# Attention with one exp per query block in place of two halves, and four buffers in place of two in the statistics pass

## The chip, the cores and the metric

The kernel runs as one program on all 8 cores of one Trainium2 chip. Each core computes 1024 tokens of the output; nothing is exchanged between cores. The metric is the device time of the slowest core in microseconds (us).

## What is computed

One transformer layer in which attention and a mixture of experts both read the same normalised input and are added to it. Cut to what matters:

```python
xn = layernorm(x)                                  # x: (4, 2048, 2048) f32
# attention, H = 16 heads of HD = 128, G = 4 key/value groups (head h uses group h % 4)
qkv = xn @ Wqkv + bqkv
scores = einsum('bqhd,bkhd->bhqk', q, k) / HD
prob = softmax(scores, axis=-1)                    # over 2048 keys
attn = einsum('bhqk,bkhd->bqhd', prob, v) @ Wout + bout
# 32 experts of width 768, top 8 of a softmax gate, with a threshold
for each expert e: acc += (silu(xn @ Wg[e].T) * (xn @ Wu[e].T)) @ Wd[e].T * combine[:, e]
out = x + attn + acc
```

## The kernel before

Each core owns 1024 tokens of one sequence (x_own) and also reads the other 1024 (x_nbr), for keys and values. Every engine has its own instruction list in program order; semaphores written out by hand order them (one counter each for TensorE, VectorE and ScalarE, `st`, `sv`, `ss`, and one per DMA buffer). On VectorE and ScalarE each instruction also waits for the one before it. The stages, in order:

1. **Statistics pass** (L286 to L300). For 16 tiles of 128 tokens: SP loads 128x2048 f32 (1 MB) into one of the two buffers `xtile`, VectorE sums it (L296), ScalarE squares it with a running sum into PSUM that nobody reads (L299). SP may refill a buffer when both engines are done with the tile two back. L302 to L318 then turn the 16 sums into mean and scale with small VectorE instructions and one square root.
2. **Normalising pass** (L422 to L531). The same 16 tiles are loaded again, normalised by ScalarE (L439, L443), transposed on TensorE (L457, L482) and copied out; the gate's logits (L498), then the QKV matmuls (L351).
3. **Attention** (L596 to L732), 128 blocks i = (head h, query block q of 128), eight blocks a head. `ps_a` is four banks of PSUM, 128x2048 f32, one block's scores against all 2048 keys. For block i the engines are given:
   - TensorE: scores of the keys 0 to 1023 (L616) once the first exp of block i-1 is done, scores of 1024 to 2047 (L627) once the second exp is done; in every eighth block the 32 P·V matmuls of the head before (L703); then 16 transposes of the normalised block i-2 into `ps_b` (L675).
   - VectorE: the copy of `ps_b` into `pnT` for block i-2 (L689), then, for block i, the add of the two halves' sums (L651), a running offset (L657), a reciprocal (L659), and the normalising multiply into `pn_sb` (L662).
   - ScalarE: where P·V was done, its two copies out (L712); the exp of the first half (L643) and of the second (L647), each with an accumulated row sum, which costs an accumulator read behind it; then Ln of the whole sum (L654), for which it waits on VectorE's add. Offset and `p_exp` are double buffered: the exp of block i waits for VectorE's L657 and L662 of block i-2.
4. **Output projection** (L753) and the **expert stage** (L858 to L931), the bulk of the time: gate and up matmuls (L895), down matmuls (L831) with weights streamed by GpSimd's queue.
5. The final transposes, the residual and the store.

`B.barrier()` stands between attention and its neighbours: all engines wait for TensorE, VectorE and ScalarE. GpSimd's queue issues nothing during attention; SP's issues nothing either.

Of the kernel before, what the change touches and what calls it, by code (L numbers as in the profile page):

```python
# [102 lines left out]
def build_program():  # L103
# [18 lines left out]
    def sb(name, shape, dtype, off):  # L122
        return nc.alloc_sbuf_tensor_at(name, shape, dtype, offset=MBASE + off).ap()
# [23 lines left out]
    sm = Small(8192, 16384)  # L147
# [12 lines left out]
    nmax128 = sm.get("nmax128", 1)  # L160
    ssum = sm.get("ssum", 1)
    ssum2 = [sm.get("ssum2a", 1), sm.get("ssum2b", 1)]
    ssb2 = [sm.get("ssb2a", 1), sm.get("ssb2b", 1)]
    lns2 = [sm.get("lns2a", 1), sm.get("lns2b", 1)]
    nmax2 = [sm.get("nmax2a", 1), sm.get("nmax2b", 1)]
    rssum = sm.get("rssum", 1)
# [22 lines left out]
    sumx_all = sm.get("sumx_all", 16)  # L189
    sumx2_all = sm.get("sumx2_all", 16)  # L190
# [19 lines left out]
    xtile = [sb(f"xtile{i}", [128, D], F32, DYN + i * 8192) for i in range(2)]  # L210
# [38 lines left out]
    ps_a = nc.alloc_psum_tensor("ps_a", [128, 2048], F32).ap()  # L249
# [4 lines left out]
    B = Builder(nc)  # L254
# [17 lines left out]
    ev_xdma = [None] * 16  # L272
    ev_red1 = [None] * 16
    ev_sq1 = [None] * 16
# [8 lines left out]
    ev_cT = [None] * 16  # L283
    ev_cTev = [None] * 16

    for t in range(16):  # L286
        own = t < 8
        buf = t % 2
        src_ = dx_own if own else dx_nbr
        row = (t % 8) * 128  # L290
        if t >= 2:
            B.wait("sync", "sv", ev_red1[t - 2])
            B.wait("sync", "ss", ev_sq1[t - 2])
        ev_xdma[t] = B.dma("sync", xtile[buf][:], src_[row:row + 128, :], f"sxt{buf}")
        B.wait("vector", f"sxt{buf}", ev_xdma[t])
        ev_red1[t] = B.op("vector", lambda e, b=buf, t=t: e.reduce_sum(  # L296
            sumx_all[:, t:t + 1], xtile[b][:], axis=AX.X), "sv")
        B.wait("scalar", f"sxt{buf}", ev_xdma[t])
        ev_sq1[t] = B.op("scalar", lambda e, b=buf, t=t: e.activation(  # L299
            ps_a[:, 0:2048], xtile[b][:], AF.Square, accum_out=sumx2_all[:, t:t + 1]), "ss")  # L300

    B.wait("vector", "ss", ev_sq1[15])  # L302
    B.op("vector", lambda e: e.tensor_scalar_mul(mean_all[:], sumx_all[:], 1.0 / D))
# [118 lines left out]
    for t in range(16):  # L422
        own = t < 8
        buf = t % 2
        src_ = dx_own if own else dx_nbr
        row = (t % 8) * 128
        if t >= 2:
            B.wait("sync", "ss", ev_xn_done[t - 2])
        else:
            B.wait("sync", "sv", ev_red1[14 + t])  # L430
            B.wait("sync", "ss", ev_sq1[14 + t])
        ev_xdma[t] = B.dma("sync", xtile[buf][:], src_[row:row + 128, :], f"sxt{buf}")

        B.wait("scalar", f"sxt{buf}", ev_xdma[t])
        if t >= 2:
            B.wait("scalar", "st", ev_tpb[t - 2][1])
            if t - 2 < 8:
                B.wait("scalar", "st", ev_tpf[t - 2][1])
        ev_xnbf[t] = B.op("scalar", lambda e, b=buf, t=t: e.activation(  # L439
            xnbf[b][:], xtile[b][:], AF.Identity,  # L440
            bias=negmr_all[:, t:t + 1], scale=rstd_all[:, t:t + 1]), "ss")
        if own:
            ev_xnf[t] = B.op("scalar", lambda e, b=buf, t=t: e.activation(  # L443
                xnf[b][:], xtile[b][:], AF.Identity,
                bias=negmr_all[:, t:t + 1], scale=rstd_all[:, t:t + 1]), "ss")
# [147 lines left out]

    B.barrier()

    ev_expAC = [None] * 128  # L596
    ev_expBC = [None] * 128
    ev_normC = [None] * 128
    ev_biasC = [None] * 128
    ev_tpC = {}  # L600
# [7 lines left out]
    def emit_scores(i):  # L608
        h, q = divmod(i, 8)
        g = h % G  # L610
        if i >= 1:
            B.wait("tensor", "ss", ev_expAC[i - 1])

        def sc_mm01(e, h=h, q=q, g=g):
            for kb in range(2):
                ins = e.matmul(ps_a[:, kb * 512:(kb + 1) * 512],  # L616
                               q_sb[:, h * TOWN + q * 128: h * TOWN + q * 128 + 128],
                               k_sb[:, g * S + kb * 512: g * S + kb * 512 + 512],
                               start=True, stop=True)
            return ins  # L620
        ev01 = B.op("tensor", sc_mm01, "st")
        if i >= 1:
            B.wait("tensor", "ss", ev_expBC[i - 1])

        def sc_mm23(e, h=h, q=q, g=g):
            for kb in (2, 3):
                ins = e.matmul(ps_a[:, kb * 512:(kb + 1) * 512],  # L627
                               q_sb[:, h * TOWN + q * 128: h * TOWN + q * 128 + 128],
                               k_sb[:, g * S + kb * 512: g * S + kb * 512 + 512],
                               start=True, stop=True)  # L630
            return ins
        ev23 = B.op("tensor", sc_mm23, "st")
        return (ev01, ev23)

    def emit_softmax(i, ev_sc):
        qb2 = i % 2
        B.wait("scalar", "st", ev_sc[0])
        if i >= 2:
            B.wait("scalar", ev_normC[i - 2][0], ev_normC[i - 2][1])
            B.wait("scalar", "sv", ev_biasC[i - 2])  # L640
        else:
            B.wait("scalar", "sv", ev_nz)
        ev_expAC[i] = B.op("scalar", lambda e, qb2=qb2: e.activation(  # L643
            p_exp[qb2][:, 0:1024], ps_a[:, 0:1024], AF.Exp, bias=nmax2[qb2][:],
            accum_out=ssum2[qb2][:]), "ss")
        B.wait("scalar", "st", ev_sc[1])
        ev_expBC[i] = B.op("scalar", lambda e, qb2=qb2: e.activation(  # L647
            p_exp[qb2][:, 1024:2048], ps_a[:, 1024:2048], AF.Exp, bias=nmax2[qb2][:],
            accum_out=ssb2[qb2][:]), "ss")
        B.wait("vector", "ss", ev_expBC[i])  # L650
        ev_stot = B.op("vector", lambda e, qb2=qb2: e.tensor_tensor(  # L651
            ssum2[qb2][:], ssum2[qb2][:], ssb2[qb2][:], ALU.add), "sv")
        B.wait("scalar", "sv", ev_stot)
        ev_ln = B.op("scalar", lambda e, qb2=qb2: e.activation(  # L654
            lns2[qb2][:], ssum2[qb2][:], AF.Ln), "ss")
        B.wait("vector", "ss", ev_ln)
        ev_biasC[i] = B.op("vector", lambda e, qb2=qb2: e.tensor_tensor(  # L657
            nmax2[qb2][:], nmax2[qb2][:], lns2[qb2][:], ALU.subtract), "sv")
        B.op("vector", lambda e, qb2=qb2: e.reciprocal(rssum[:], ssum2[qb2][:]))  # L659
        if (i - 2, 1) in ev_tpC:  # L660
            B.wait("vector", ev_tpC[(i - 2, 1)][0], ev_tpC[(i - 2, 1)][1])
        ev_normC[i] = ("sv", B.op("vector", lambda e, qb2=qb2: e.tensor_scalar_mul(  # L662
            pn_sb[qb2][:], p_exp[qb2][:], rssum[:]), "sv"))
# [194 lines left out]
    for e in range(NE):  # L858
        B.wait("tensor", f"ssel{e % 2}", ev_sel[e])
        for hfi in range(2):  # L860
            if ev_crep_psfree is not None:
# [4 lines left out]
                start=True, stop=True), "st")  # L866
# [167 lines left out]
```

How the kernel before makes its waits and increments, by code:

```python
    def op(self, eng, fn, inc=None, n=1):  # L43
        auto = self.SELF_SEM.get(eng)
        if auto is not None:
            assert inc in (None, auto), (eng, inc)
            self.wait(eng, auto, self.cnt[auto])
            inc = auto
            n = 1
        if inc is None:
            self.streams[eng].append(lambda e, fn=fn: fn(e))
            return None
        self.cnt[inc] += n
        sem = self.sems[inc]
        self.streams[eng].append(
            lambda e, fn=fn, sem=sem, n=n: fn(e).then_inc(sem, n))
        return self.cnt[inc]
# [4 lines left out]
    def wait(self, eng, semname, val):  # L62
        if val is None or val <= 0:
            return
        self.streams[eng].append(
            lambda e, s=self.sems[semname], v=val: e.wait_ge(s, v))
```

## Time and profile before

| | us |
|---|---|
| three runs, median | 5870.77 |
| lowest, highest | 5581.49, 6046.8 |
| the profiled execution | 5581.49 |
| its span, slowest core (core 4) | 5579.6 |
| spans of the eight cores | 5564.0 to 5579.6 |
| mean granted TensorE clock of the cores | 0.955 to 0.958 |

The profiled execution is the lowest of the three. All rows come from core 4 of it. A row of the timeline is start and duration in us, engine, line, operation, output<-inputs, and in brackets how long the engine sat idle before it and what ended that. PE is TensorE, PEld its weight loads, DVE VectorE, ACT ScalarE. The end of a matmul row is modelled. The granted clock is a share of full speed, and a few matmul records can be missing (a group of 32 may be listed as x31).

### The profile page before, as it was taken

What the parts mean: (1) busy time and instruction counts of PE and PEld (TensorE: products, weight loads), DVE (VectorE), ACT (ScalarE), POOL (GpSimd) and SP (SyncE); (2) the same over time, 40 slices, a digit from 0 to 9 for tenths busy, and PEclk for the clock granted to TensorE, in tenths of its full rate; (3) what the DMA queues carried; (4) which work ended last, traced back from release to release, by engine and by line L of the source; (5) the groups of instructions that cost most, each with busy time, mean ns of one, the idle gap of its engine ahead of it and who ended that gap; (6) DMA issues with size and microseconds to landing.
All of it is one profiled execution on the core that took longest, in us unless ns stands there. A gap on an engine that the chain in (4) does not pass through costs nothing.

```text
span 5579.6 us, 64195 instructions; the slowest of 8 cores (5564.0 to 5579.6 us)
## 1 busy us (share of the span) xinstructions
PE 5010.6 (90%) x23550; PEld 2328.6 (42%) x24008; DVE 1741.9 (31%) x2616; ACT 792.5 (14%) x1301; POOL 261.6 (5%) x497
## 2 busy tenths in 40 slices
PE   3875666678999999999999999999999999999995
PEld 2532333333444444444444444444444444444443
DVE  3002566630233322222222233332222222223333
ACT  4221555531000000000000000000000000000000
POOL 0000000000000000000000000000000000000000
PEclk9787999989999999999999999999999999999997
DMA  5231000016434444444444433434444444444333
GB/s 172 73 75 31 1 1 1 1 21 105 76 68 75 74 73 79 72 75 73 74 74 72 76 72 69 78 71 77 75 72 76 72 76 72 75 74 72 68 63 123
DMA packets 80462, 380.45 MB, mean 68 GB/s; under 512 B 9760, under 2 KB 10912, under 8 KB 65824
## 3 DMA queue, kind: packets, MB, share of 16 engines
q0 software_dynamic: 70992, 325.12, 33.0%
q1 hardware_dynamic: 9168, 51.21, 2.7%
q8 instruction: 201, 3.29, 0.2%
q14 instruction: 101, 0.83, 0.1%
HBM read 693.00 MB, written 8.39 MB: 126 GB/s over the span
## 4 chain that ended last, share of the span: by engine, by line
PE 83%; DVE 8%; issue 3%; DMA 3%; ACT 2%; DVEq 0%; ACTq 0%; SPq 0%; POOLq 0%
PE ps_a L895 48%; PE ps_d L831 23%; PE ps_a L351 4%; DVE pn_sb L662 2%; DVE pnT L689 2%; PE ps_d L703 2%; PE ps_a L753 2%; PE ps_b L863 1%; PE ps_b L498 1%; DMA x_re<-x_own 1%; DMA wgubuf<-gu 1%; PE ps_b L457 1%; PE ps_d L482 0%; ACT p_exp L647 0%; DMA xtile<-x_own 0%
## 5 line engine op out<-in xcount | busy, mean ns | idle before, releaser
L895 PE MATMUL ps_a<-xn_own,wgubuf 128*128 128x512 bf16 x12044 | 2692.8, 384 | 24.6 <-DMA wgubuf<-gu 10.8
L895 PEld LDWEIGHTS ps_a<-xn_own,wgubuf 128*128 128x128 bf16 x12288 | 1211.4, 99 | 1517.4 <-issue 103.7
L831 PE MATMUL ps_d<-hstash,wdbuf 128*128 128x512 bf16 x6016 | 1330.5, 379 | 11.1 <-DVE ffn_acc L841 0.9
L918 DVE TENSOR_TENSOR sg_sb<-ps_a,sg_sb 128x512 f32<-128x512 f32 x384 | 265.6, 692 | 2408.2 <-PE ps_a L895 2408.2
L831 PEld LDWEIGHTS ps_d<-hstash,wdbuf 128*128 128x128 bf16 x6144 | 596.0, 97 | 741.5 <-issue 181.8
L841 DVE TENSOR_TENSOR ffn_acc<-ffn_acc,ps_d 128x512 f32<-128x512 f32 x1024 | 703.8, 687 | 606.7 <-PE ps_d L831 603.0
L908 ACT ACTIVATE sg_sb<-ps_a 128x512 f32<-128x512 f32 x384 | 229.3, 597 | 2260.1 <-PE ps_a L895 2260.1
L60 POOL DMA_DIRECT2D wgubuf<-gu x384 | 203.5, 530 | 2602.6 <-PE ps_a L895 2546.8
L923 DVE TENSOR_TENSOR hstash<-sg_sb,c_rep 128x512 bf16<-128x512 f32 x384 | 266.0, 693 | 39.9
L873 ACT ACTIVATE c_rep<-ps_b 128x512 f32<-128x512 f32 x64 | 38.2, 597 | 1534.9 <-PE ps_b L863 1485.8
L689 DVE COPY pnT<-ps_b 128x2048 bf16<-128x2048 bf16 x128 | 156.7, 1224 | 115.2 <-PE ps_b L675 103.3
L351 PE MATMUL ps_a<-xn_own,wjbuf 128*128 128x512 bf16 x750 | 181.4, 404 | 2.4 <-issue 1.8
L616 PE MATMUL ps_a<-k_sb,q_sb 128*128 128x512 bf16 x214 | 75.0, 419 | 110.4 <-ACT p_exp L643 108.0
L662 DVE TENSOR_SCALAR pn_sb<-p_exp,rssum 128x2048 bf16<-128x2048 f32 x128 | 164.6, 1286 | 14.5 <-DVE rssum L659 1.2
L675 PE MATMUL ps_b<-ident_b,pn_sb 128*128 128x128 bf16 x2048 | 149.5, 231 | 17.2 <-DVE pnT L689 8.0
L675 PEld LDWEIGHTS ps_b<-ident_b,pn_sb 128*128 128x128 bf16 x2048 | 131.4, 104 | 71.1 <-issue 64.2
L627 PE MATMUL ps_a<-k_sb,q_sb 128*128 128x512 bf16 x256 | 81.6, 402 | 80.5 <-ACT p_exp L647 80.5
L457 PE MATMUL ps_b<-ident_b,xnbf 128*128 128x128 bf16 x256 | 30.2, 291 | 124.1 <-ACT xnbf L439 107.9
L703 PE MATMUL ps_d<-pnT,vt_sb 128*128 128x512 bf16 x501 | 125.9, 411 | 8.0 <-DVE ssum2b L651 4.8
L351 PEld LDWEIGHTS ps_a<-xn_own,wjbuf 128*128 128x128 bf16 x768 | 79.2, 104 | 101.8 <-issue 24.3
L753 PE MATMUL ps_a<-attn_o,woutbuf 128*128 128x512 bf16 x502 | 113.1, 386 | 7.3 <-DMA woutbuf<-wout 6.7
L351 PE MATMUL ps_a<-xn_nbr,wjbuf 128*128 128x512 bf16 x251 | 58.0, 389 | 55.4 <-DMA wjbuf<-wqkv 55.0
(106 smaller groups left out, 1302.4 us busy)
## 6 DMA issues: line engine op xcount, KB each, us to landing
wgubuf<-gu POOLq DMA_DIRECT2D x384, 512.0 KB, 5.0
wdbuf<-down POOLq DMA_DIRECT2D x64, 1536.0 KB, 10.8
xtile<-x_own SPq DMA_DIRECT2D x16, 1024.0 KB, 5.2
xtile<-x_nbr SPq DMA_DIRECT2D x16, 1024.0 KB, 5.7
wjbuf<-wqkv POOLq DMA_DIRECT2D x28, 512.0 KB, 6.1
woutbuf<-wout POOLq DMA_DIRECT2D x16, 512.0 KB, 5.3
x_re<-x_own SPq DMA_DIRECT2D x8, 1024.0 KB, 6.9
o<-out_sb SPq DMA_DIRECT2D x8, 1024.0 KB, 4.8
```

The source lines that it names most:

```text
L351: ins = e.matmul(ps_a[:, bank * 512:(bank + 1) * 512], wjbuf[use][:, dc * 128:(dc + 1) * 128], xn_mv(dc, tblk), start=(dc == 0), stop=(dc ...
L662: ev_normC[i] = ("sv", B.op("vector", lambda e, qb2=qb2: e.tensor_scalar_mul(pn_sb[qb2][:], p_exp[qb2][:], rssum[:]), "sv"))
L675: ins = e.matmul(ps_b[:, k * 1024 + j * 128: k * 1024 + (j + 1) * 128], pn_sb[qb2][:, kc * 128:(kc + 1) * 128], ident_b[:], is_transpose=True,
L689: e.tensor_copy(d, s), "sv")
L703: ins = e.matmul(pv_ps, vt_sb[:, (g * 16 + kc) * 128:(g * 16 + kc) * 128 + 128], pnT[:, kc * TOWN + qb * 512: kc * TOWN + qb * 512 + 512], ...
L753: ins = e.matmul(ps_a[:, bank * 512:(bank + 1) * 512], woutbuf[oc % 2][:, dic * 128:(dic + 1) * 128], attn_o[:, dic * TOWN + tblk * 512: d ...
L831: ins = e_.matmul(ps_d[:, slot * 512:(slot + 1) * 512], wdbuf[gh % 3][:, (dc % 8) * 768 + icc * 128: (dc % 8) * 768 + icc * 128 + 128], hs ...
L841: e_.tensor_tensor(ffn_acc[:, dc * TOWN + tb * 512: dc * TOWN + tb * 512 + 512], ffn_acc[:, dc * TOWN + tb * 512: dc * TOWN + tb * 512 + 512],
L895: ins = e_.matmul(ps_a[:, bank * 512:(bank + 1) * 512], wgubuf[bufi][:, dc * 128:(dc + 1) * 128], xn_own[:, dc * TOWN + tb * 512: dc * TOW ...
L908: ev_silu[(e, ip, tb)] = B.op("scalar", lambda e_, tb=tb: e_.activation(sg_sb[:, tb * 512:(tb + 1) * 512], ps_a[:, tb * 512:(tb + 1) * 512 ...
L918: ev_h1[(e, ip, tb)] = B.op("vector", lambda e_, tb=tb: e_.tensor_tensor(sg_sb[:, tb * 512:(tb + 1) * 512], ps_a[:, (2 + tb) * 512:(3 + tb ...
L923: e_.tensor_tensor(hstash[e2 % 2][:, ip * TOWN + tb * 512: ip * TOWN + tb * 512 + 512], sg_sb[:, tb * 512:(tb + 1) * 512], c_rep[e2 % 2][: ...
```

## The change

Three edits.

- **Statistics pass.** Two more 1 MB buffers, `xp1a` and `xp1b`, laid over memory that the normalising pass uses later (`xnf1` and `xnTf0`), join `xtile`; tile t goes to buffer t % 4, each with its own semaphore, and SP waits for the tile four back. The first two reloads of the normalising pass wait for tiles 12 and 13, and ScalarE's first normalise also waits for the last reduction.
- **Scores.** The two groups of two matmuls per block become one of four, which waits for the whole exp of the block before.
- **Softmax.** The two exps of 1024 columns become one of 2048 with one accumulated sum; the second sum, VectorE's add and ScalarE's wait for it are gone.

```diff
--- before.py
+++ after.py
@@ -160,7 +160,6 @@
     nmax128 = sm.get("nmax128", 1)
     ssum = sm.get("ssum", 1)
     ssum2 = [sm.get("ssum2a", 1), sm.get("ssum2b", 1)]
-    ssb2 = [sm.get("ssb2a", 1), sm.get("ssb2b", 1)]
     lns2 = [sm.get("lns2a", 1), sm.get("lns2b", 1)]
     nmax2 = [sm.get("nmax2a", 1), sm.get("nmax2b", 1)]
     rssum = sm.get("rssum", 1)
@@ -219,6 +218,9 @@
     act_all = sb("act_all", [128, 8 * NE], F32, 193536)
     scr_all = sb("scr_all", [128, 8 * NE], F32, 194560)
     fb_all = sb("fb_all", [128, 8 * NE], F32, 195584)
+    xp1 = [None, None,
+           sb("xp1a", [128, D], F32, 49152),
+           sb("xp1b", [128, D], F32, 57344)]
     xn_own = sb("xn_own", [128, DC * TOWN], BF16, 73728)
     xn_nbr = sb("xn_nbr", [128, DC * TOWN], BF16, 106496)
 
@@ -283,21 +285,23 @@
     ev_cT = [None] * 16
     ev_cTev = [None] * 16
 
+    xp1[0], xp1[1] = xtile[0], xtile[1]
+    p1sem = ["sxt0", "sxt1", "sxr0", "sxr1"]
     for t in range(16):
         own = t < 8
-        buf = t % 2
+        buf = t % 4
         src_ = dx_own if own else dx_nbr
         row = (t % 8) * 128
-        if t >= 2:
-            B.wait("sync", "sv", ev_red1[t - 2])
-            B.wait("sync", "ss", ev_sq1[t - 2])
-        ev_xdma[t] = B.dma("sync", xtile[buf][:], src_[row:row + 128, :], f"sxt{buf}")
-        B.wait("vector", f"sxt{buf}", ev_xdma[t])
+        if t >= 4:
+            B.wait("sync", "sv", ev_red1[t - 4])
+            B.wait("sync", "ss", ev_sq1[t - 4])
+        ev_xdma[t] = B.dma("sync", xp1[buf][:], src_[row:row + 128, :], p1sem[buf])
+        B.wait("vector", p1sem[buf], ev_xdma[t])
         ev_red1[t] = B.op("vector", lambda e, b=buf, t=t: e.reduce_sum(
-            sumx_all[:, t:t + 1], xtile[b][:], axis=AX.X), "sv")
-        B.wait("scalar", f"sxt{buf}", ev_xdma[t])
+            sumx_all[:, t:t + 1], xp1[b][:], axis=AX.X), "sv")
+        B.wait("scalar", p1sem[buf], ev_xdma[t])
         ev_sq1[t] = B.op("scalar", lambda e, b=buf, t=t: e.activation(
-            ps_a[:, 0:2048], xtile[b][:], AF.Square, accum_out=sumx2_all[:, t:t + 1]), "ss")
+            ps_a[:, 0:2048], xp1[b][:], AF.Square, accum_out=sumx2_all[:, t:t + 1]), "ss")
 
     B.wait("vector", "ss", ev_sq1[15])
     B.op("vector", lambda e: e.tensor_scalar_mul(mean_all[:], sumx_all[:], 1.0 / D))
@@ -427,11 +431,13 @@
         if t >= 2:
             B.wait("sync", "ss", ev_xn_done[t - 2])
         else:
-            B.wait("sync", "sv", ev_red1[14 + t])
-            B.wait("sync", "ss", ev_sq1[14 + t])
+            B.wait("sync", "sv", ev_red1[12 + t])
+            B.wait("sync", "ss", ev_sq1[12 + t])
         ev_xdma[t] = B.dma("sync", xtile[buf][:], src_[row:row + 128, :], f"sxt{buf}")
 
         B.wait("scalar", f"sxt{buf}", ev_xdma[t])
+        if t == 0:
+            B.wait("scalar", "sv", ev_red1[15])
         if t >= 2:
             B.wait("scalar", "st", ev_tpb[t - 2][1])
             if t - 2 < 8:
@@ -593,8 +599,7 @@
 
     B.barrier()
 
-    ev_expAC = [None] * 128
-    ev_expBC = [None] * 128
+    ev_expC = [None] * 128
     ev_normC = [None] * 128
     ev_biasC = [None] * 128
     ev_tpC = {}
@@ -609,48 +614,28 @@
         h, q = divmod(i, 8)
         g = h % G
         if i >= 1:
-            B.wait("tensor", "ss", ev_expAC[i - 1])
-
-        def sc_mm01(e, h=h, q=q, g=g):
-            for kb in range(2):
+            B.wait("tensor", "ss", ev_expC[i - 1])
+
+        def sc_mm(e, h=h, q=q, g=g):
+            for kb in range(4):
                 ins = e.matmul(ps_a[:, kb * 512:(kb + 1) * 512],
                                q_sb[:, h * TOWN + q * 128: h * TOWN + q * 128 + 128],
                                k_sb[:, g * S + kb * 512: g * S + kb * 512 + 512],
                                start=True, stop=True)
             return ins
-        ev01 = B.op("tensor", sc_mm01, "st")
-        if i >= 1:
-            B.wait("tensor", "ss", ev_expBC[i - 1])
-
-        def sc_mm23(e, h=h, q=q, g=g):
-            for kb in (2, 3):
-                ins = e.matmul(ps_a[:, kb * 512:(kb + 1) * 512],
-                               q_sb[:, h * TOWN + q * 128: h * TOWN + q * 128 + 128],
-                               k_sb[:, g * S + kb * 512: g * S + kb * 512 + 512],
-                               start=True, stop=True)
-            return ins
-        ev23 = B.op("tensor", sc_mm23, "st")
-        return (ev01, ev23)
+        return B.op("tensor", sc_mm, "st")
 
     def emit_softmax(i, ev_sc):
         qb2 = i % 2
-        B.wait("scalar", "st", ev_sc[0])
+        B.wait("scalar", "st", ev_sc)
         if i >= 2:
             B.wait("scalar", ev_normC[i - 2][0], ev_normC[i - 2][1])
             B.wait("scalar", "sv", ev_biasC[i - 2])
         else:
             B.wait("scalar", "sv", ev_nz)
-        ev_expAC[i] = B.op("scalar", lambda e, qb2=qb2: e.activation(
-            p_exp[qb2][:, 0:1024], ps_a[:, 0:1024], AF.Exp, bias=nmax2[qb2][:],
+        ev_expC[i] = B.op("scalar", lambda e, qb2=qb2: e.activation(
+            p_exp[qb2][:], ps_a[:], AF.Exp, bias=nmax2[qb2][:],
             accum_out=ssum2[qb2][:]), "ss")
-        B.wait("scalar", "st", ev_sc[1])
-        ev_expBC[i] = B.op("scalar", lambda e, qb2=qb2: e.activation(
-            p_exp[qb2][:, 1024:2048], ps_a[:, 1024:2048], AF.Exp, bias=nmax2[qb2][:],
-            accum_out=ssb2[qb2][:]), "ss")
-        B.wait("vector", "ss", ev_expBC[i])
-        ev_stot = B.op("vector", lambda e, qb2=qb2: e.tensor_tensor(
-            ssum2[qb2][:], ssum2[qb2][:], ssb2[qb2][:], ALU.add), "sv")
-        B.wait("scalar", "sv", ev_stot)
         ev_ln = B.op("scalar", lambda e, qb2=qb2: e.activation(
             lns2[qb2][:], ssum2[qb2][:], AF.Ln), "ss")
         B.wait("vector", "ss", ev_ln)
```

## Rows read from the trace of the kernel before

**Rows 1.** The page: the chain that ended last, share of the span by line.

```profile
PE ps_a L895 48%; PE ps_d L831 23%; PE ps_a L351 4%; DVE pn_sb L662 2%; DVE pnT L689 2%; PE ps_d L703 2%; PE ps_a L753 2%; PE ps_b L863 1%; PE ps_b L498 1%; DMA x_re<-x_own 1%; DMA wgubuf<-gu 1%; PE ps_b L457 1%; PE ps_d L482 0%; ACT p_exp L647 0%; DMA xtile<-x_own 0%
```

**Rows 2.** Statistics pass: groups by line, landing times, timeline, a window's busy times.

```profile
L296 DVE TENSOR_REDUCE sumx_all<-xtile 128x1 f32<-128x2048 f32 x16 | 36.6, 2286 | 31.5 <-DMA xtile<-x_own 17.2 <-DMA xtile<-x_nbr 14.3
L299 ACT ACTIVATE ps_a<-xtile 128x2048 f32<-128x2048 f32 x16 | 30.1, 1881 | 29.1 <-DMA xtile<-x_nbr 16.1 <-DMA xtile<-x_own 12.9
...
DMA to landing us min/median/max: 4.8/5.4/10.7
...
12.20 2.29 DVE L296 TENSOR_REDUCE sumx_all<-xtile 128x1 f32<-128x2048 f32 x1 [4.97 <-DMA xtile<-x_own]
21.53 2.29 DVE L296 TENSOR_REDUCE sumx_all<-xtile 128x1 f32<-128x2048 f32 x1 [4.52 <-DMA xtile<-x_own]
72.98 2.29 DVE L296 TENSOR_REDUCE sumx_all<-xtile 128x1 f32<-128x2048 f32 x1 [2.34 <-DMA xtile<-x_nbr]
79.41 2.09 ACT L439 ACTIVATE xnbf<-xtile,negmr_all,rstd_all 128x2048 bf16<-128x2048 f32 x1 [1.95 <-DVE negmr_all L317]
...
21.00:39.00 18.00, 0.00 (x0) 0.00 (x0) 11.38 (x5) 10.01 (x10) 0.00 (x0) 1.00 0.80 266
```

**Rows 3.** Timeline of one block of the attention loop (start, us, instruction).

```profile
725.45 1.11 ACT L643 ACTIVATE p_exp<-ps_a,nmax2a 128x1024 f32<-128x1024 f32 x1
...
727.76 0.19 ACT L647 ACTIVATION_READ_ACCUMULATOR p_exp<-ps_a,nmax2a 128x1 f32 x1
728.10 0.59 PE L627 MATMUL ps_a<-k_sb,q_sb 128*128 128x512 bf16 x2 [0.70 <-ACT p_exp L647]
728.78 0.16 DVE L651 TENSOR_TENSOR ssum2a<-ssum2a,ssb2a 128x1 f32<-128x1 f32 x1
729.39 1.11 ACT L643 ACTIVATE p_exp<-ps_a,nmax2b 128x1024 f32<-128x1024 f32 x1
729.47 0.16 DVE L657 TENSOR_TENSOR nmax2a<-nmax2a,lns2a 128x1 f32<-128x1 f32 x1 [0.52 <-ACT lns2a L654]
730.00 1.29 DVE L662 TENSOR_SCALAR pn_sb<-p_exp,rssum 128x2048 bf16<-128x2048 f32 x1
731.39 1.23 DVE L689 COPY pnT<-ps_b 128x2048 bf16<-128x2048 bf16 x1
732.72 0.16 DVE L651 TENSOR_TENSOR ssum2b<-ssum2b,ssb2b 128x1 f32<-128x1 f32 x1
```

**Rows 4.** Who waited for whom, attention stage (us in total, times, longest us).

```profile
PE ps_a L616 <- ACT p_exp L643: 105.9, 113, 1.5
...
ACT lns2b L654 <- DVE ssum2b L651: 70.8, 62, 1.5
```

**Rows 5.** Timeline of the block with the P·V matmuls and the next.

```profile
732.98 7.07 PE L703 MATMUL ps_d<-pnT,vt_sb 128*128 128x512 bf16 x31 [0.24 <-DVE ssum2b L651]
...
740.20 0.60 ACT L712 ACTIVATE attn_o<-ps_d 128x512 bf16<-128x512 f32 x1 [2.86 <-PE ps_d L703]
740.88 1.11 ACT L643 ACTIVATE p_exp<-ps_a,nmax2a 128x1024 f32<-128x1024 f32 x1
...
743.96 1.05 PE L675 MATMUL ps_b<-ident_b,pn_sb 128*128 128x128 bf16 x16
744.16 1.12 ACT L643 ACTIVATE p_exp<-ps_a,nmax2b 128x1024 f32<-128x1024 f32 x1
```

**Rows 6.** Busy times by stretch, attention stage (last three: PEclk, DMA share, GB/s).

```profile
575.00:1216.00 641.00, 424.04 (x3019) 217.27 (x3072) 383.46 (x643) 353.70 (x672) 0.18 (x1) 0.91 0.00 1
```

**Rows 7.** Timeline: a ScalarE copy-out of 1024 columns of PSUM.

```profile
86.54 1.02 ACT L489 ACTIVATE xnTf<-ps_d 128x1024 f32<-128x1024 f32 x1 [2.85 <-PE ps_d L482]
```

**Rows 8.** Timeline: the attention stage's start, and a later P·V group.

```profile
575.50 1.01 PE L616 MATMUL ps_a<-k_sb,q_sb 128*128 128x512 bf16 x2 [1.12 <-DVE vt_sb L420]
576.73 1.11 ACT L643 ACTIVATE p_exp<-ps_a,nmax2a 128x1024 f32<-128x1024 f32 x1 [4.82 <-PE ps_a L616]
...
1165.34 8.75 PE L703 MATMUL ps_d<-pnT,vt_sb 128*128 128x512 bf16 x32
```

## The prediction

> **What bounds the kernel now.** I read the page first. The chain that ended last runs for 71% of the span through the expert matmuls at L895 and L831, which the change doesn't touch [rows 1]. Both halves of the change lie outside them, in the first 1.2 ms, so I went to the groups, waits, windows and timeline of each stage there.
>
> Stage one is the statistics pass. The last tile's VectorE reduction starts at 72.98 us and the first normalising ACTIVATE at 79.41 us, 6.4 us behind it; TensorE has nothing to do before that, so every us saved there moves the end. VectorE works 2.29 us a tile, yet it sits idle for 31.5 us before these reductions, behind the DMA of x, and a load takes 5.4 us at the median from issue to landing [rows 2]. From tile 2 (21.53 us) to tile 15 (72.98 us) it is 51.45 us for 13 tiles, 3.96 us each. That is the round trip of one of two buffers, (5.4 + 2.3 + some 0.2 of signals) / 2 = 3.95, and not an engine.
>
> Stage two is the attention loop, 575.5 to about 1216 us [rows 6, 8], 640 us. In its steady part one block of 128 queries takes 732.72 - 728.78 = 3.94 us [rows 3]. VectorE sets it: from its L651 through the Ln on ScalarE to L657 is 0.69 us, then 0.53 with L659 to L662, 1.39 to L689 and 1.33 to the next L651: 3.94. The only hole in it is the 0.52 us for the Ln. ScalarE's Ln waits for VectorE's sum (70.8 us in one of its two buffers' turns), TensorE for the exps (105.9 us for the first half alone) [rows 4]. The eighth block is longer: the P·V matmuls stand between, 7.07 us, and ScalarE's next exp is queued behind their copy-out. From exp to exp that block takes 740.88 - 729.39 = 11.49 us, the next one 3.28 us (VectorE had caught up) [rows 5]. A head is thus 11.49 + 3.28 + 6 x 3.94 = 38.4 us at full clock; the mean over the 11 heads from the P·V at 732.98 [rows 5] to that at 1165.34 [rows 8] is 432.4 / 11 = 39.3 us. The other 0.9 us are stretches at a lower granted clock: 0.91 over the stage [rows 6], that is (of the levels 2.4 and 1.2 GHz) about 18% of the time at the low one.
>
> **Part 1, the statistics pass.** Four buffers in place of two; SP waits for the tile four back. The round trip no longer limits: four in flight would allow 7.9 / 4 = 2.0 us a tile. Two things are next. VectorE needs 2.29 + 0.11 = 2.40 us a tile. The DMA engines carry 266 GB/s at a busy share of 0.80 between 21 and 39 us [rows 2]; filled up, that is 266 / 0.80 = 332 GB/s, and 1.049 MB take 3.16 us. I take 3.16, because the share says the engines are nearer to full than to idle. The first tile is processed from 12.20 us as before (loads on one queue are served in order), the last from 12.2 + 15 x 3.16 = 59.6 us in place of 72.98: 13 us earlier. Bounds: nothing (the share of 0.80 already is all there is to have, 3.96 us stays), and 72.98 - (12.2 + 15 x 2.40) = 25 us (VectorE bound). The Trainium skill, "DMA: Bandwidth & Descriptors", section Specifications, gives about 358 GB/s of HBM for a core when both of a pair stream: 2.93 us a tile, an estimate by that page, which would save 17 us. The rate of [rows 2], 266 GB/s, lies well under that.
>
> The reloads of the second pass wait for tiles 12 and 13 in place of 14 and 15 and queue behind the last loads on SP; they were in time before (the normalising started on VectorE's last statistic, not on a transfer), so this is 0. The new wait of ScalarE for the last reduction costs 0: that reduction is an input of the statistics ScalarE waits for anyway.
>
> **Part 2, attention.** It removes per block one ACTIVATE's fixed part and one 0.19 us accumulator read from ScalarE, the 0.16 us add L651 from VectorE, and the trip ScalarE, VectorE, ScalarE ahead of the Ln. It adds an ordering: no score matmul of the next block may start before the whole exp is done, and no exp before all four matmuls are. Two halves of ps_a that leapfrogged become one buffer that the engines hand to and fro.
>
> The new exp, 128x2048: a copy-out of 512 columns costs 0.60 us [rows 5] and one of 1024 costs 1.02 [rows 7], 0.42 per 512. The two exps of today take 727.95 - 725.45 = 2.50 us with their reads [rows 3], 1.21 each and a gap of 0.09; one with 1024 columns more is 1.21 + 0.84 = **2.05**. Bounds: 1.88, which is the 2048-wide square without its read [rows 2], and 2.23, the copy-out's 1.02 doubled with the read's 0.19.
>
> The new loop between ScalarE and TensorE, at full clock: exp and read 2.05; to the first score matmul 0.15 (727.95 to 728.10); four matmuls: two take 0.59 [rows 3], and P·V shows 7.07 / 32 = 0.22 for one more, so 0.59 + 0.44 = 1.03; back to ScalarE 0.15 to 0.22 (P·V's end 740.05 to 740.20, the first scores' end 576.51 to 576.73 [rows 5, 8]), say 0.2. Sum **3.43 us**. The Ln (0.3 us) lies beside the matmuls. VectorE's share is 0.53 + 1.39 + 1.33 = 3.25, less than 3.43, and its order must also fit: with exp i at 0, Ln ends at 2.35, L657 starts at 2.53, L662 ends at 4.35. Behind the now later scores in TensorE's queue stand the transposes of block i-1: they run from 3.24 to 4.29 (1.05 us [rows 5]), and L689 that waits for them starts at 4.5 and ends at 5.7, before L657 of the next block is due at 3.43 + 2.53 = 5.96. VectorE has 0.2 us in hand. ScalarE needs VectorE's normalise only of two blocks back, over 2 us early. So the bound moves from VectorE to the exp-scores loop, by 0.5 us a block.
>
> Block with P·V: 2.05 + 0.15 + 1.03 + 7.1 + 0.15 + 0.60 + 0.08 = 11.2 (before 11.49). The one behind it: 3.43, 0.15 *more* than before, since it was not VectorE bound. Head: 11.2 + 7 x 3.43 = 35.2 us at full clock.
>
> The low clock now costs more, because the matmuls lie bare in the loop. Two score matmuls take 1.01 us there [rows 8] and one more 0.22 + (1.01 - 0.59) / 2 = 0.43, so four 1.86: the block is 4.26. P·V: 8.75 us where a part was low [rows 8]; all low, 32 x 0.43 = 13.7. A head all at low is 11.2 + 0.83 + 6.6 + 7 x 4.26 = 48.4. With 18% of the time low: 35.2 + 0.18 x 13.2 = 37.6, against 39.3. That is 1.7 us a head, 16 heads: **27 us**. Bounds: exp at 2.23 takes 8 x 0.18 x 16 = 23 us of it; exp at 1.88 gives 8 x 0.17 x 16 = 22 us more.
>
> **Sum.** The profiled execution took 5581.5 us (span 5579.6). 5581.5 - 13 - 27 = **5541 us**, 0.7% less. This run is the lowest of three (median 5870.8, up to 6046.8), whose spread is far over the change. The number is for an execution like the profiled one; the same ratio on the median would be 5828. A measurement of this kernel tells about 2% from no change, 112 us.
>
> **Rivals.** *A, as above*: 5541, its own range 5520 to 5560; chance 0.60.
> *B, VectorE stays the bound in attention*: its 3.25 us plus the 0.52 us it waits for the Ln if that never gets hidden, 3.77 a block. For it: only 0.2 us in hand in my order of events. Against it: the Ln no longer waits for VectorE, and exp of the next block runs on. Head 11.2 + 3.43 + 6 x 3.77 = 37.3, with the 0.9 us that the low clock costs a VectorE-bound head today 38.2: 18 us saved, 5581.5 - 13 - 18 = 5550. With the exp at its top bound instead, 5581.5 - 13 - 4 = 5564. 0.14.
> *C, TensorE's clock sinks in attention, and it gets slower.* The score matmuls at the stage's start run at 1.2 GHz (1.01 us for two, 0.59 later) [rows 3, 8], while TensorE did only short groups of them. If the longer hole (4.29 to 5.64, 1.35 us a block, now up to 1.2) holds the clock low, a head costs 35.2 + 13.2 s with s the share at low; the gain of both parts is gone at 39.3 + 13/16 = 40.1, s = 0.37, granted clock 0.81; all low is 48.4, +146 - 13 = 5714. Against it: TensorE's busy share rises, (1.03 + 1.05) / 3.43 = 61% from (1.18 + 1.05) / 3.94 = 57%. The Trainium skill, "TensorE: Matmul & The Clock Gate", section A second HAM failure mode, says that short idles between matmul groups cycling through PSUM make the clock flip to and fro, and that is this pattern; the trace agrees so far that 0.91, not 1, is granted. 0.08, half of it over 2%.
> *D, the statistics pass gives nothing*, loads only take longer as more are in flight: 5554. For it the share of 0.80. 0.11.
> *E, both go to their good bounds*: VectorE-bound statistics (-25) and a clock of 0.98 (head 35.7, -58): 5499. 0.07.
>
> Over 2% faster (5470) is past even E: 0.02. Slower by over 2% is the far half of C: 0.04. Within: 0.94. Leaving out most of C and the far side of E gives 5500 to 5580.
>
> **What would show it.** In the profile after: L296 of tile 15 at about 60 us (3.2 us a tile), SP's waits for L296 small; a DMA share near 1 in that stretch. In attention the exp line with 128x2048 at about 1.97 us, exp to exp 3.4 us, the score matmuls in fours of 1.03, ScalarE waiting for TensorE and not for VectorE, VectorE waiting a little for the Ln, 37.6 us between P·V groups, the stage about 613 us long and a granted clock near 0.91. The expert stage must keep its length. It is wrong if the blocks stay at 3.8 or more (B), if the clock is under 0.85 (C), or if tiles stay near 3.9 us (D).

## The result

The changed kernel takes 0.9894 of the time of the kernel before (95% interval 0.9878 to 0.991), about 60 us less, which is within 2%: the executions compared lie between 5514 and 5540 us, those of the kernel before between 5578 and 5584. The median over all twelve executions, 5581.9 us (before 5783.9 over fourteen), also counts those in which a die ran at a lower clock throughout, and the ratio and the times below leave these out.

The rows below are of the profiled execution (5519.7 us, span 5517.8, core 3). First the statistics pass, by the timeline (start, duration) and the busy times of a stretch (last three numbers: granted clock, DMA busy share, GB/s). They answer to [rows 2]; line 300 is the former L296, L445 the former L439.

```profile
11.69 2.29 DVE L300 TENSOR_REDUCE sumx_all<-xtile 128x1 f32<-128x2048 f32 x1 [4.38 <-DMA xtile<-x_own]
...
58.62 2.29 DVE L300 TENSOR_REDUCE sumx_all<-xp1b 128x1 f32<-128x2048 f32 x1 [1.13 <-DMA xp1b<-x_nbr]
65.09 2.09 ACT L445 ACTIVATE xnbf<-xtile,negmr_all,rstd_all 128x2048 bf16<-128x2048 f32 x1 [2.01 <-DVE negmr_all L321]
...
12.00:54.00 42.00, 0.00 (x0) 0.00 (x0) 30.80 (x14) 28.32 (x28) 0.00 (x0) 1.00 1.00 342
```

A tile now takes (58.62 - 11.69) / 15 = 3.13 us in place of 3.96. The DMA engines are full (a busy share of 1.00), and the first normalise comes at 65.09 in place of 79.41: 14.3 us.

Next, one steady block of attention by the timeline, to be laid beside [rows 3]. L621 is the scores, L636 the exp, L639 the Ln, L642 the offset, L647 the normalise, L660 the transposes, L674 their copy.

```profile
734.94 1.97 ACT L636 ACTIVATE p_exp<-ps_a,nmax2a 128x2048 f32<-128x2048 f32 x1 [1.14 <-PE ps_a L621]
735.90 1.22 DVE L674 COPY pnT<-ps_b 128x2048 bf16<-128x2048 bf16 x1
736.81 0.19 ACT L636 ACTIVATION_READ_ACCUMULATOR p_exp<-ps_a,nmax2a 128x1 f32 x1
737.09 0.20 ACT L639 ACTIVATE lns2a<-ssum2a 128x1 f32<-128x1 f32 x1
...
737.14 1.02 PE L621 MATMUL ps_a<-k_sb,q_sb 128*128 128x512 bf16 x4 [1.57 <-ACT p_exp L636]
737.47 0.16 DVE L642 TENSOR_TENSOR nmax2a<-nmax2a,lns2a 128x1 f32<-128x1 f32 x1 [0.34 <-ACT lns2a L639]
...
738.00 1.29 DVE L647 TENSOR_SCALAR pn_sb<-p_exp,rssum 128x2048 bf16<-128x2048 f32 x1
738.00 1.06 PE L660 MATMUL ps_b<-ident_b,pn_sb 128*128 128x128 bf16 x16
738.43 1.97 ACT L636 ACTIVATE p_exp<-ps_a,nmax2b 128x2048 f32<-128x2048 f32 x1 [1.14 <-PE ps_a L621]
```

From exp to exp it is 738.43 - 734.94 = 3.49 us, where it was 3.94. ScalarE and TensorE hand the four banks to and fro with no gap but the two signals between them (0.14 and 0.27 us), and VectorE has 0.34 us to spare. The waits over the stage (total, times, longest) say the same. Where ScalarE waited for VectorE's sum [rows 4], it now waits for the scores:

```profile
PE ps_a L621 <- ACT p_exp L636: 198.6, 127, 2.4
ACT p_exp L636 <- PE ps_a L621: 126.7, 98, 5.7
```

The block with P·V (timeline; L688 the matmuls, L697 the copy-out), beside [rows 5], and, two blocks behind it, a block at the low clock:

```profile
701.89 1.97 ACT L636 ACTIVATE p_exp<-ps_a,nmax2b 128x2048 f32<-128x2048 f32 x1 [1.14 <-PE ps_a L621]
...
704.95 7.07 PE L688 MATMUL ps_d<-pnT,vt_sb 128*128 128x512 bf16 x32
...
712.86 1.97 ACT L636 ACTIVATE p_exp<-ps_a,nmax2a 128x2048 f32<-128x2048 f32 x1
...
716.66 1.97 ACT L636 ACTIVATE p_exp<-ps_a,nmax2b 128x2048 f32<-128x2048 f32 x1 [1.44 <-PE ps_a L621]
...
718.86 1.86 PE L621 MATMUL ps_a<-k_sb,q_sb 128*128 128x512 bf16 x4 [0.76 <-ACT p_exp L636]
...
720.99 1.97 ACT L636 ACTIVATE p_exp<-ps_a,nmax2a 128x2048 f32<-128x2048 f32 x1 [1.98 <-PE ps_a L621]
```

The P·V block is 712.86 - 701.89 = 10.97 us (before 11.49 at full clock), the low-clock block 720.99 - 716.66 = 4.33. The stage's busy times and granted clock, beside [rows 6], and the stage behind it:

```profile
558.00:1149.00 591.00, 383.55 (x3072) 230.39 (x3072) 363.61 (x515) 308.60 (x416) 0.64 (x2) 0.94 0.00 1
1149.00:5517.00 4368.00, 4250.21 (x19200) 1901.52 (x19200) 1255.44 (x1808) 290.84 (x481) 244.22 (x463) 0.98 0.42 76
```

The account of the profiled pair; the first two columns are times from the start of the span, the last is what the stage itself gained:

| up to | before | after | gained in the stage |
|---|---|---|---|
| first normalise | 79.41 | 65.09 | 14.3 |
| first scores of attention | 575.50 | 558.89 | 2.3 |
| last copy-out of attention begins | 1214.68 | 1147.23 | 50.8 |
| end of the span | 5579.6 | 5517.8 | -5.6 |

The ends of those stages, before (core 4) and after (core 3), by the timeline:

```profile
1214.68 0.60 ACT L712 ACTIVATE attn_o<-ps_d 128x512 bf16<-128x512 f32 x1 [2.86 <-PE ps_d L703]
...
558.89 1.86 PE L621 MATMUL ps_a<-k_sb,q_sb 128*128 128x512 bf16 x4 [1.12 <-DVE vt_sb L424]
...
1147.23 0.60 ACT L697 ACTIVATE attn_o<-ps_d 128x512 bf16<-128x512 f32 x1 [2.86 <-PE ps_d L688]
```

The table compares one core with another. In the mean over the eight cores of the two executions the four gains are 14.0, -0.5, 50.7 and -3.2 us, so the 2.3 is a difference between cores. The stages behind attention, which the change doesn't touch, took 4362 us in the mean of the cores before and 4366 after; in the profiled executions of e3 to e9 they took 4363 (e4) to 4369 us (e3), so the last line is no larger than what executions differ by.

One more thing changed that no row above shows alone. Of the 15 P·V groups that have a block behind them, 7 took 8.6 to 8.8 us before on core 4 (5 to 7 on the other cores), the others 7.1. After the change all 15 take 7.1, on every one of the eight cores.

### The profile page after: what moved, and what is told of

It is laid out like the page before. It is cut to its first block, busy times and chain, and to the rows that moved or that the text cites. A ratio compares the mean times of both kernels' runs of the same rounds, so it can differ in the third digit from the quotient of the medians.

```text
span 5517.8 us, 63499 instructions; the slowest of 8 cores (5503.0 to 5517.8 us)
## 1 busy us (share of the span) xinstructions
PE 4991.4 (90%) x24008; PEld 2341.2 (42%) x24008; DVE 1722.2 (31%) x2488; ACT 747.5 (14%) x1045; POOL 260.5 (5%) x497
## 4 chain that ended last, share of the span: by engine, by line
PE 87%; ACT 6%; DMA 3%; DVE 2%; issue 2%; ACTq 0%; SPq 0%; DVEq 0%; POOLq 0%
PE ps_a L880 49%; PE ps_d L816 24%; ACT p_exp L636 4%; PE ps_a L355 4%; PE ps_a L621 2%; PE ps_d L688 2%; PE ps_a L738 2%; PE ps_b L848 1%; DMA x_re<-x_own 1%; PE ps_b L504 1%; DMA wgubuf<-gu 1%; PE ps_b L463 1%; PE ps_d L488 1%; DMA xp1b<-x_nbr 0%; DVE out_sb L948 0%
## 5 line engine op out<-in xcount | busy, mean ns | idle before, releaser
L621 PE MATMUL ps_a<-k_sb,q_sb 128*128 128x512 bf16 x512 | 142.7, 404 | 199.7 <-ACT p_exp L636 198.6
L674 DVE COPY pnT<-ps_b 128x2048 bf16<-128x2048 bf16 x128 | 156.8, 1225 | 135.7 <-PE ps_b L660 125.8
L647 DVE TENSOR_SCALAR pn_sb<-p_exp,rssum 128x2048 bf16<-128x2048 f32 x128 | 164.7, 1287 | 14.9 <-PE ps_a L621 1.4
L660 PEld LDWEIGHTS ps_b<-ident_b,pn_sb 128*128 128x128 bf16 x2048 | 137.6, 104 | 39.0 <-issue 14.8
L660 PE MATMUL ps_b<-ident_b,pn_sb 128*128 128x128 bf16 x2048 | 148.9, 231 | 4.2 <-DVE pnT L674 4.1
L621 PEld LDWEIGHTS ps_a<-k_sb,q_sb 128*128 128x128 bf16 x512 | 42.3, 99 | 255.6 <-issue 228.0
L636 ACT ACTIVATE p_exp<-ps_a,nmax2b 128x2048 f32<-128x2048 f32 x64 | 125.9, 1968 | 79.9 <-PE ps_a L621 73.7
L636 ACT ACTIVATE p_exp<-ps_a,nmax2a 128x2048 f32<-128x2048 f32 x64 | 126.0, 1969 | 66.4 <-PE ps_a L621 53.0
```

The source lines that it names most:

```text
L621: ins = e.matmul(ps_a[:, kb * 512:(kb + 1) * 512], q_sb[:, h * TOWN + q * 128: h * TOWN + q * 128 + 128], k_sb[:, g * S + kb * 512: g * S ...
L636: ev_expC[i] = B.op("scalar", lambda e, qb2=qb2: e.activation(p_exp[qb2][:], ps_a[:], AF.Exp, bias=nmax2[qb2][:], accum_out=ssum2[qb2][:]) ...
L660: ins = e.matmul(ps_b[:, k * 1024 + j * 128: k * 1024 + (j + 1) * 128], pn_sb[qb2][:, kc * 128:(kc + 1) * 128], ident_b[:], is_transpose=True,
```

## The experiments

The kernel before took 5585.6 to 5589 us beside e1 to e7, and 5582 to 5589 beside e8 and e9. The questions were: do the two halves of the change add; is the round trip through VectorE what bounded the block; what do the halves of the exp and the score group give or cost; and what freed P·V from the low clock.

**The two halves apart.** e1_stats_only is the kernel before with the statistics pass of the changed one. e2_attn_only is the changed kernel with the statistics pass of before:

```diff
-    buf = t % 4
+    buf = t % 2
-    if t >= 4: wait for tile t-4
+    if t >= 2: wait for tile t-2
```

> Only the statistics pass has four buffers; attention is that of before. Theory (two separate gains that add): the last tile's reduction at about 58.6 us as in the changed kernel (3.13 us a tile), the first normalise 14.3 us earlier than before, the whole about 14 to 17 us shorter, 5565 us (ratio 0.997). The P·V groups stay as mixed as before, some 6 of 15 at 8.5 to 8.8 us. Rival (the freed time in front shifts the phase of the granted clock and that is what keeps P·V at full clock in the changed kernel): P·V groups all at 7.1 us and another 10 us saved, 5555 us.

> Only the attention half of the change, statistics pass with two buffers. Theory: blocks of 3.49 us, P·V blocks of 10.97, P·V groups never at the low clock, the attention stage 589 us in place of 640, the whole about 50 us shorter: 5531 us (ratio 0.991). Rival (phase of the clock from the shorter front): P·V groups slow in some heads, the stage about 599 us, the whole 40 us shorter, 5541 us.

e1 took 5570.0 to 5574.3 us in three executions (before 5585.7 and 5587.8): 15 us less in the mean, the theory's figure for the transfer gain, and not the rival's 5555. Its profiled execution took 6357.5 us at a granted clock of 0.83, so it doesn't answer the question on P·V; e2 does. e2 took 5533.6 and 5536.2, 52 us less. On cores 4 to 7 of its profile (granted clock 0.96) the blocks are 3.49, the P·V blocks 10.97, and no P·V group with a block behind it is slow, although the front is as long as before. So the halves add (15 + 52 against 66 for the whole in e7 below, on another chip whose kernel before took the same 5587), and the phase of the front is not what changed the clock.

**Joined scores alone.** The four matmuls in one group that waits for the second exp; two exps, add and round trip as before:

```diff
-        if i >= 1: B.wait("tensor", "ss", ev_expAC[i - 1])
-        ... two matmuls ...
         if i >= 1: B.wait("tensor", "ss", ev_expBC[i - 1])
-        ... two matmuls ...
+        ... four matmuls ...
```

> Kernel before with one edit: the four score matmuls in one group that waits for both exps of the block before. Two exps, VectorE's add and the Ln's wait for it stay. Theory (VectorE with the Ln's round trip is what bounds the blocks): steady blocks stay at 3.94 us, since exps, scores and signals are 2.50 + 0.15 + 1.03 + 0.2 = 3.9; the block behind P·V goes from 3.28 to 3.9; the whole 5 to 15 us longer (ratio 1.001 to 1.003) unless P·V now always gets the full clock, which would take 10 us back. Rival (the joined group is where the gain comes from): blocks near 3.5 us and 30 us or more saved.

5614.7 and 5617.4 us, 29 us *more* than before. The steady block is 3.94, so joining gives nothing by itself, as the theory said. (The loop of exps and scores is by the theory's sum nearly as long, 3.9, so this run alone doesn't tell which of the two loops holds the block.) Its low-clock blocks are 4.78, and there are more of them. Timeline and busy times of its attention:

```profile
717.51 1.12 ACT L632 ACTIVATE p_exp<-ps_a,nmax2a 128x1024 f32<-128x1024 f32 x1 [1.02 <-DVE rssum L648]
...
720.16 1.86 PE L616 MATMUL ps_a<-k_sb,q_sb 128*128 128x512 bf16 x4 [1.56 <-ACT p_exp L636]
...
728.87 1.02 PE L616 MATMUL ps_a<-k_sb,q_sb 128*128 128x512 bf16 x4 [2.02 <-ACT p_exp L636]
...
577.00:1245.00 668.00, 422.39 (x3015) 261.62 (x3068) 383.32 (x640) 353.95 (x672) 0.00 (x0) 0.83 0.00 1
```

The granted clock sank from 0.91 to 0.83 over the stage, and P·V is slow in 5 of 15. I had expected 5 to 15 us: the blocks behind P·V give 15 x 0.65 = 10 of them. The clock is the rest: what this core's blocks took over their full-clock length is 35 us, against 14 in the kernel before.

**The round trip alone.** Halves kept, but the Ln is taken of the first half's sum. The offset that it feeds only keeps the exp in range and cancels in the softmax, so ScalarE waits for no add. The offset also moves behind the normalise (edit in words):

```diff
-        ssum2 = ssum2 + ssb2 (vector); wait scalar for it; Ln(ssum2)
-        offset; reciprocal(ssum2); normalise
+        Ln(ssum2) right behind the second exp
+        ssb2 = ssum2 + ssb2 (vector); reciprocal(ssb2); normalise; offset
```

> Kernel before, exps and scores still in halves, but Ln is taken of the first half's sum (the offset it feeds cancels in the softmax), so ScalarE waits for no add; VectorE adds the halves, takes the reciprocal, normalises, copies and does the offset last. Theory: VectorE bound without the round trip, 0.26 + 0.27 + 1.39 + 1.33 + 0.26 = 3.51 us a block, the block behind P·V about 2.9 to 3.3, a head 35.5 to 36.3 us, the whole 45 to 55 us shorter, 5530 us (ratio 0.991), as much as the changed kernel's attention without giving up the halves. If the clock in P·V hangs on the joined scores, P·V stays mixed here. Rival (only the saved fixed part of the second exp matters): blocks stay at 3.8 or more, under 20 us saved.

5532.3 and 5529.1 us, 56 us less: a little more than the changed kernel's attention gives. Its steady block is 3.51 by VectorE alone, as summed. Timeline around a P·V group, and the stage:

```profile
719.28 0.16 DVE L653 TENSOR_TENSOR ssb2a<-ssum2a,ssb2a 128x1 f32<-128x1 f32 x1
...
722.79 0.16 DVE L653 TENSOR_TENSOR ssb2b<-ssum2b,ssb2b 128x1 f32<-128x1 f32 x1
723.05 7.07 PE L702 MATMUL ps_d<-pnT,vt_sb 128*128 128x512 bf16 x32 [1.82 <-DVE ssb2b L653]
...
576.00:1165.00 589.00, 388.96 (x3087) 210.09 (x3088) 384.83 (x644) 353.54 (x672) 0.00 (x0) 0.95 0.00 1
```

Exp and scores run ahead of VectorE in the first blocks of a head (2.89 us each), and are held back later; P·V then waits 1.8 us, which makes that block 12.97. (The row names the add behind it, but what the program has P·V wait for is VectorE's last copy into `pnT`.) A head is 35.9 us. So VectorE with the round trip was the bound: with the trip taken away in another way than the change does, and two exps and two score groups kept, the gain is the same. P·V is slow in 2 of 15 here, with the halves apart.

**The block's length and the clock.** The changed kernel with a useless 512-column copy on ScalarE ahead of each exp:

```diff
+        B.op("scalar", lambda e: e.activation(
+            wjbuf[0][:, 512:1024], wjbuf[0][:, 0:512], AF.Copy), "ss")
         ev_expC[i] = B.op("scalar", ...)
```

> The changed kernel with one useless 512-column copy on ScalarE ahead of each exp, behind the wait for the scores; TensorE's work is the same. Theory (TensorE's granted clock in attention follows how much of a block it works, so the changed kernel's short blocks are what freed P·V from the low clock): blocks of 3.49 + 0.5 = 4.0 us, granted clock in attention down from 0.94 to 0.83 to 0.88, some P·V groups at 8.4 us or more, low-clock blocks of 4.8. The whole 8 x 0.5 x 16 = 64 us longer plus 10 to 25 us of clock, 5595 to 5610 us. Rival (the clock follows the form, one exp and joined scores, not the length): clock stays 0.94, P·V always 7.1 us, 5585 us.

5652.9 and 5662.0 us, +1.3% to the kernel before and 43 to 67 us over what I expected. The copy costs 0.72 a block and not 0.5 (0.63 of itself and the 0.09 to the next), so blocks are 4.21, and 5.05 at the low clock. The low clock costs this core 53 us by the same count that gives 12 for the changed kernel, where I had allowed 10 to 25 more. Timeline and stage:

```profile
654.91 8.49 PE L690 MATMUL ps_d<-pnT,vt_sb 128*128 128x512 bf16 x32
...
1181.56 1.97 ACT L638 ACTIVATE p_exp<-ps_a,nmax2a 128x2048 f32<-128x2048 f32 x1
1183.43 0.19 ACT L638 ACTIVATION_READ_ACCUMULATOR p_exp<-ps_a,nmax2a 128x1 f32 x1
...
1183.76 1.87 PE L621 MATMUL ps_a<-k_sb,q_sb 128*128 128x512 bf16 x4 [1.48 <-ACT p_exp L638]
...
1186.62 1.97 ACT L638 ACTIVATE p_exp<-ps_a,nmax2b 128x2048 f32<-128x2048 f32 x1
...
560.00:1270.00 710.00, 455.96 (x3032) 274.89 (x3032) 362.31 (x515) 387.89 (x542) 0.00 (x0) 0.79 0.00 1
```

TensorE does the same matmuls as in the changed kernel, with one exp and joined scores, and yet the granted clock is 0.79 in place of 0.94, and P·V is slow (7.6 to 8.8 us) in 10 of 15. So with the form held, the length of the block moves the clock: the same TensorE work in a block of 4.21, 3.94 (e3) and 3.49 us gives 0.79, 0.83 and 0.94. The rival isn't empty, though. At the same 3.94 us the halves of the kernel before have 0.91 and the joined scores of e3 0.83, so the form moves the clock too. In e3 TensorE stands idle once in a full-clock block, for 2.02 us (its row at 728.87); before it was twice, for 1.07 and 0.70:

```profile
727.02 0.38 PE L616 MATMUL ps_a<-k_sb,q_sb 128*128 128x512 bf16 x1 [1.07 <-ACT p_exp L643]
728.10 0.59 PE L627 MATMUL ps_a<-k_sb,q_sb 128*128 128x512 bf16 x2 [0.70 <-ACT p_exp L647]
```

The six loops stand in the same order by granted clock as by the share of the block in which TensorE works, so no run here separates the length, the single pause and that share from each other. Slow P·V groups fall with the length in either form: in the joined one 10, 5 and 0 of 15 at 4.21, 3.94 and 3.49 us, in halves 7, 2 and 0 at 3.94, 3.51 and 3.26 us (the kernel before, e4, and e5 below).

**A version that keeps both.** Statistics pass of the change, attention of e4, and the offset's subtract on GpSimd, which does nothing in attention (edit against e4, in words):

```diff
-        wait vector for Ln; nmax2 = nmax2 - lns2 on vector
+        wait gpsimd for Ln; nmax2 = nmax2 - lns2 on gpsimd
```

> Four buffers in the statistics pass, and attention as in e4 (halves kept, Ln of the first half's sum) with the offset's subtract moved from VectorE to GpSimd, which is idle in attention. Theory (VectorE bounds e4's blocks): 0.26 + 0.27 + 1.39 + 1.33 = 3.25 us a block, heads 2.1 us shorter than e4's 35.9, 34 us in all, and 14.6 us from the statistics: 5531 - 34 - 15 = 5482 us, ratio 0.981 to the kernel before, 0.993 to the changed one. Granted clock in attention at or above e4's 0.96. Rival (GpSimd's subtract is late and holds up the exp two blocks on): blocks at 3.5 or more, 5515 us.

5482.6 to 5487.4 us in three executions: ratio 0.9817 (0.9796 to 0.9838) to the kernel before, 36 us under the changed one. VectorE's add comes every 3.26 us when it is the bound, and the subtract costs 0.19 us on GpSimd, for which the exp waited only 9 times in the stage, 4.1 us in all. No P·V group with a block behind it is slow, on any core (timeline, stage):

```profile
717.86 0.16 DVE L661 TENSOR_TENSOR ssb2a<-ssum2a,ssb2a 128x1 f32<-128x1 f32 x1
...
719.96 0.19 POOL L670 TENSOR_TENSOR nmax2b<-nmax2b,lns2b 128x1 f32<-128x1 f32 x1 [2.70 <-ACT lns2b L658]
...
721.12 0.16 DVE L661 TENSOR_TENSOR ssb2b<-ssum2b,ssb2b 128x1 f32<-128x1 f32 x1
...
560.00:1119.00 559.00, 385.77 (x3035) 209.89 (x3088) 364.45 (x516) 353.20 (x673) 24.62 (x128) 0.96 0.00 1
```

**Buffers of the statistics pass.** Three and eight in place of four; the changed kernel again as the measure.

```diff
-        buf = t % 4
+        buf = t % 3      # e6;  t % 8 in e9
```

> The changed kernel with three buffers in the statistics pass in place of four. Theory (with the round trip gone the DMA engines bound it): three in flight hide (5.4 + 2.4) / 3 = 2.6 us a tile, under the 3.13 of the transfers, so the last tile's reduction stays within 1.5 us of 58.6 and the time within 2 us of the changed kernel. Rival (every buffer in flight still buys bandwidth): about 3.4 us a tile, 4 us later, and 4 us more in all.

> The changed kernel with eight buffers in the statistics pass. Theory (transfers bound it, at a DMA busy share of 1.0 and 342 GB/s): 3.1 us a tile as with four, the last reduction at 57.5 to 59 us, the time within 2 us of the changed kernel. Rival (more in flight buys more bandwidth, as from two to four): the last reduction at about 50 us, VectorE bound, 8 us saved.

> The changed kernel unaltered, on the same chip as the two others, as their measure: 5521 us where the kernel before takes 5583 (ratio 0.989).

The same stretch, 12 to 54 us, first with three buffers (e6), then with eight (e9; core 0 of each):

```profile
12.00:54.00 42.00, 0.00 (x0) 0.00 (x0) 28.45 (x13) 26.35 (x26) 0.00 (x0) 1.00 0.98 311
```

```profile
12.00:54.00 42.00, 0.00 (x0) 0.00 (x0) 30.86 (x14) 28.08 (x29) 0.00 (x0) 1.00 1.00 341
```

With eight the last reduction of the cores starts at 57.6 to 59.4 us, with four at 57.5 to 58.6: nothing gained, the transfers are the bound. With three it is 61.0 to 63.2, 3.40 us a tile on core 0, and the kernel took 5527.4 to 5528.0 against 5519.0 to 5522.6 of e7. That is the rival's figure, and my theory was wrong there. But e7's own profiled execution, with the four buffers of the change, had its last reductions at 59.0 to 61.4 (328 to 331 GB/s, where the first profile had 337 to 342, at the same busy share). So three buffers cost 2 to 4 us in this pass; the rest of the 6 us in the times isn't in it. e9's times spread from 5523.7 to 5568.5 us and settle nothing. e7 itself repeats the result, ratio 0.9882.

## Why the prediction was right or wrong

- **What bounds the statistics pass** (round trip of two buffers, then the transfers): right. Forecast 3.16 us a tile and 13 us; measured 3.13 and 14.3; eight buffers confirm the bound. Some of the closeness is luck: e7, the same kernel, took 3.22 to 3.37 us a tile. The estimate from 266 GB/s at a share of 0.80 came out because the engines did fill up, to 342 GB/s at 1.00. The Trainium skill's 358 GB/s ("DMA: Bandwidth & Descriptors", Specifications) was not reached; the measured rate decides.
- **What bounds attention** (VectorE with the Ln's round trip): right, by e4, which removes the trip, keeps the halves and comes down to 3.51, and in keeping with e3, which removes none of it and stays at 3.94.
- **The new loop**: forecast 3.43, measured 3.49. The exp is 1.97 start to end, 2.06 with its read (forecast 2.05); the scores 1.02 (1.03); the signals were 0.14 and 0.27 where I took 0.15 and 0.2. "ScalarE: Activation LUTs" of the Trainium skill (What ACT_TABLE_LOAD costs) gives 280 ns + 0.833 ns an element for an ACTIVATE with a per-partition bias. That is 1.99 us here, an estimate by that page, and the row's 1.97 agrees. VectorE's hand-free time was forecast at 0.2, measured 0.34. P·V block: 11.2, measured 10.97, since P·V starts 0.86 us behind the first score matmul and not 1.03. A head at full clock: 35.2, measured 10.97 + 7 x 3.49 = 35.4.
- **The size of the low clock's price: wrong, and it is the term that failed.** I put 18% of the time at the low level, unchanged from before, at 13.2 us a head: 2.4 us a head, 38 in all. Measured is what the blocks of the profiled core took over their full-clock length: (3.578 - 3.49) x 97 = 8.5 us in the ordinary blocks, 3.4 in those behind P·V, 0 in P·V: 12 us. Three things were wrong in one step. The share was multiplied with a price per full-clock head, though a share of *time* at the low level holds less work: 1 / (0.82 / 35.2 + 0.18 / 48.4) = 37.0 us a head, 29 us in all and not 38. The share was kept from before, but it fell to 12% (clock 0.94), which makes the term 19. And the low stretches were spread evenly, P·V's 6.6 us included; they never fell on it, which makes the term 11, by an estimate from these rows. The same count before the change is 12 us on P·V alone and 14 in all. So the low clock costs 12 after and 14 before, where I had it cost 24 more.
- **The sum**: 13 + 27 against 14.3 + 50.8. Of the 24 us that attention gave over the forecast, 26 are the low clock's price (38 forecast, 12 measured), less 16 x 0.2 = 3 for the longer full-clock head. From one P·V group to the next it is 36.1 us (forecast 37.6), the stage 591 us (613). Total forecast 5541 (0.9928 of before), the profiled execution took 5519.7 (0.9889 of the profiled one before). That is in the range of 5500 to 5580, at the low edge of A's own 5520 to 5560, halfway to E. The median over all executions, 5581.9, lies just outside the range. The prediction named the spread of the three times before, up to 6046.8, but its range had no room for it: it was for an execution like the profiled one.
- **The rivals.** B (VectorE stays the bound) fell: its waits for the Ln are 0.34 a block and off the path. C (the clock sinks) was wrong in sign for this change, but the mechanism exists: e8, with 0.72 us more of idle TensorE in each block, has exactly that, a clock of 0.79 and a kernel slower than before. My argument against C, a larger share of the block with TensorE at work, fits all the runs, though none tests it apart from the length; I did not carry it into the sum. "TensorE: Matmul & The Clock Gate" of the Trainium skill (A second HAM failure mode) warns of short idles between matmul groups; the traces agree in that the clock does flip (score groups of 1.02 and of 1.86 us), but the changed kernel idles 1.57 us in one piece ahead of its scores, longer than either pause of before (1.07 and 0.70), and has the higher clock. D fell: 14.3 us came. E's clock part was nearly there in time (51 of its 58 us), though the clock went to 0.94 and not to 0.98.

## What to carry to other kernels

Where two engines hand a buffer to and fro and a third stands in the loop for one tiny result, price the round trip, not the instruction: 0.16 us of VectorE work cost 0.43 us a block (3.94 against 3.51 in e4, which still does the work). Look then whether the result is needed there at all: taking the Ln of what is already at hand (e4, e5) gives at least as much as merging the work (56 against 52 us), keeps the overlap, and lets one more step move to an idle engine (e5). When a change shortens a loop that TensorE shares, don't carry the old low-clock share into the sum, and ask on which matmuls the low stretches will fall. When it lengthens one, count the clock too: 0.72 us more a block took the granted clock from 0.94 to 0.79 besides.

## What the runs showed of the hardware

- The granted clock of a mixed loop moves with the loop's length at equal TensorE work: 4.21, 3.94 and 3.49 us gave 0.79, 0.83 and 0.94; with the scores in halves 3.94, 3.51 and 3.26 us gave 0.91, 0.95 and 0.96. At equal length, 3.94 us, one group of scores gave 0.83 and two gave 0.91. How the low stretches choose their place stays open: after the change they lie mostly in one or two of the three blocks behind P·V, before it on P·V itself in 7 of 15 heads.
- Sixteen transposes take 1.05 us at the high level and 1.86 at the low one, like matmuls; after the change about 110 of the 128 groups ran wholly at the high level (core 3).
- An exp of 2048 columns from four PSUM banks costs no more per column than one of 1024: 1.97 against 1.11 us, 0.86 for 1024 columns more.
- Loads of 1 MB on one queue: between 12 and 54 us the cores moved 242 and 254 GB/s with two in flight (cores 4 and 0; 266 in the stretch of [rows 2]), 301 to 313 with three, 328 to 342 with four (two executions) and 339 to 342 with eight, all eight cores loading.
